# Turning the context rows of two pairs of heads' steps together: one PSUM bank, one reciprocal and one product in place of two of each

## The reference

```
q = (x @ Wq) 32 heads of 8;  k, v = (x @ Wk), (x @ Wv) 8 heads of 8;  rope(q), rope(k)
scores = q k^T / sqrt(8), causal;  attn = softmax(scores)
ctx = attn @ v                       # (8 batches, 256 tokens, 32 heads, 8)
x = x + layernorm(ctx.reshape(b, T, 256) @ Wo + b_out)
x = x + layernorm(ffn(layernorm(x))) # 8 experts, top 2, and 2 shared ones
```

## Time and profile before

| what | value |
|---|---|
| median of 3 runs | 658.25 us (657.97 to 658.33) |
| the profiled execution: its own time | 659.02 us |
| its span in the trace | 657.1 us |
| TensorE (PE) busy | 631.5 us, 96% |
| VectorE (DVE) busy | 531.3 us, 81% |
| ScalarE (ACT) busy | 423.2 us, 64% |
| GpSimd (POOL) busy | 333.6 us, 51% |

### The profile page before, as it was taken

The page is one execution under the profiler, slowest core; times in us unless marked ns, Lnnn a source line. Parts: engine busy times, 40 slices in busy tenths (PEclk is TensorE's granted clock), DMA queues, the critical chain, the costliest instruction groups (busy, mean ns, idle before and its releaser), DMA issues.

```text
span 657.1 us, 15356 instructions
## 1 busy us (share of the span) xinstructions
PE 631.5 (96%) x5934; PEld 518.5 (79%) x5934; DVE 531.3 (81%) x1055; ACT 423.2 (64%) x798; POOL 333.6 (51%) x528
## 2 busy tenths in 40 slices
PE   8997899999999979999999999999999999999995
PEld 6854456666655547888899999999999999888884
DVE  5699999999998744479879888888988888558886
ACT  2437788889887875542257876787877787422222
POOL 3227667877766761100275454545454530078864
PEclk9998999999999999999999999999999999999998
DMA  3953633655540000000367786877776864032311
GB/s 91 177 128 77 107 84 70 131 111 145 112 88 12 19 10 17 17 1 1 120 234 257 248 279 212 266 245 255 242 265 234 260 220 153 25 91 83 94 56 64
DMA packets 79671, 87.10 MB, mean 133 GB/s; under 512 B 54352, under 2 KB 69072, under 8 KB 79600
## 3 DMA queue, kind: packets, MB, share of 16 engines
q0 software_dynamic: 11872, 54.53, 25.1%
q1 hardware_dynamic: 67312, 31.08, 19.3%
q10 hardware_dynamic: 416, 0.52, 0.3%
HBM read 63.83 MB, written 9.31 MB: 111 GB/s over the span
## 4 chain that ended last, share of the span: by engine, by line
PE 79%; DVE 12%; issue 3%; ACT 3%; POOL 2%; SPq 1%; DMA 1%; POOLq 0%; DVEq 0%; ACTq 0%
PE PS L553 75%; DVE NM L1073 3%; DVE NM L1069 2%; PE PS L564 2%; PE PS L760 1%; ACT PF L922 1%; POOL PF L1491 1%; DVE X L1338 1%; DVE RR L1034 1%; PE PS L708 1%; DMA X<-in_x 1%; DVE RA L1027 1%; ACT WH L869 0%; POOL RS L1434 0%; SPq L1593 0%
## 5 line engine op out<-in xcount | busy, mean ns | idle before, releaser
L1278 DVE TENSOR_TENSOR HF<-SS,PS 128x256 f32<-128x256 f32 (+2 forms) x141 | 68.6, 487 | 66.7 <-ACT SS L968 37.9
L1357 DVE TENSOR_TENSOR WL<-RAW,WH 128x768 fp32r<-128x768 f32 x125 | 118.4, 958 | 4.4 <-ACT WH L869 4.1
L968 ACT ACTIVATE SS<-PS 128x256 f32<-128x256 f32 (+2 forms) x141 | 62.0, 440 | 79.2 <-PE PS L553 77.5
L869 ACT ACTIVATE HH<-HF 128x256 fp32r<-128x256 f32 (+1 forms) x120 | 58.0, 483 | 72.6 <-DVE HF L1278 70.3
L1491 POOL TENSOR_SCALAR_AFFINE_SELECT PF<-PF 128x512 f32<-128x512 f32 x128 | 83.1, 674 | 41.5 <-ACT PF L922 41.3
L869 ACT ACTIVATE WH<-RAW 128x768 fp32r<-128x768 f32 x125 | 103.3, 841 | 0.0
L553 PE MATMUL PS<-WH,HH 128*128 128x256 f32 x355 | 103.2, 291 | 0.2
L553 PE MATMUL PS<-WL,HH 128*128 128x256 f32 x355 | 100.3, 282 | 0.0
L553 PE MATMUL PS<-WH,HL 128*128 128x256 f32 x355 | 100.2, 282 | 0.0
L922 ACT ACTIVATE PF<-PS 128x1536 f32<-128x1536 f32 x64 | 92.8, 1449 | 11.4 <-PE PS L553 10.1
L553 PE MATMUL PS<-XGL,WH 128*128 128x256 f32 x320 | 90.5, 283 | 0.0
(11 more groups left out here) (212 smaller groups left out, 1488.3 us busy)
## 6 DMA issues: line engine op xcount, KB each, us to landing
ys<-YO SPq DMA_DIRECT2D x16, 256.0 KB, 3.1
RAW<-in_wsh SPq DMA_DIRECT2D x4, 768.0 KB, 4.6
XT<-in_xt SPq DMA_DIRECT2D x8, 256.0 KB, 3.3
X<-in_x SPq DMA_DIRECT2D x8, 256.0 KB, 3.3
xn<-YY SPq DMA_DIRECT2D x16, 128.0 KB, 1.7
out<-X SPq DMA_DIRECT2D x15, 128.0 KB, 1.7
ys<-YO SPq DMA_DIRECT2D x7, 128.0 KB, 2.3
RAW<-in_wsh SPq DMA_DIRECT2D x2, 384.0 KB, 5.1
```

Source lines behind the costliest of these rows:

```text
L869: return eng.activation(o, i, ACT.Copy)
L968: eng.activation(ss, both(i, bank(b))[0], ACT.Silu).then_inc(free[b] if dense(i) else silu, 1)
L1278: eng.tensor_tensor(hf, ss, both(c, bank(b))[1], ALU.mult).then_inc(free[b], 1)
L1357: eng.tensor_tensor(WL[q % 2][:, c], RAW[raw_of(q)][:, c], WH[q % 2][:, c].bitcast(F32), ALU.subtract).then_inc(w_lo, 1)
```

## The change

The divide of pair 2k, with its back, no longer has a place of its own. When two pairs are copied, one back with four transposes puts both into one whole bank, and one divide of 32 sums and 256 values follows. `CTX` is laid out as two halves of four heads' steps each, and b_turn reads two blocks of 128 from it.

```
@@ plan
-            if o == "v":
-                out.extend(("back", k) for k in pairs)
-                divided.extend(pairs)
+            if o == "v" and len(pairs) == 2:
+                out.append(("back", pairs[0] // 2))
+                divided.append(pairs[0] // 2)
                 pairs.clear()
@@ build
-        CTX = sb("CTX", [P, 2, 2, 256], F32, behind)
+        CTX = sb("CTX", [P, 2, 2, 2, 128], F32, behind)
-        RC = ab("RC", [P, 2, 8], F32)
+        RC = ab("RC", [P, 32], F32)
@@ tensor
                 elif what == "back":
-                    e.wait_ge(ev, i + 1)
+                    e.wait_ge(ev, 2 * i + 2)
                     e.wait_ge(d_cf, 16)
-                    half_turn(s, YC[:, i % 2, :], identf)
+                    c = take(s)
+                    for m in range(2):
+                        for T in range(2):
+                            at = 256 * T + 128 * m
+                            t = eng.transpose(bank(c, at, at + 128), YC[:, m, 128 * T:128 * T + 128], identf)
+                    t.then_inc(full[c], 1)
                 elif what == "b_turn":
-                    for k in range(4):
-                        read(e, ("back", 4 * (i // 2) + k))
-                    half_turn(s, CTX[:, i // 2 % 2, i % 2, :], identf)
+                    for k in range(2):
+                        read(e, ("back", 2 * (i // 2) + k))
+                    c = take(s)
+                    for k in range(2):
+                        t = eng.transpose(bank(c, 128 * k, 128 * k + 128), CTX[:, i // 2 % 2, k, i % 2, :], identf)
+                    t.then_inc(full[c], 1)
@@ scalar, weighed
-                    made(e, ("back", h - 2))
+                    made(e, ("back", h // 2 - 1))
@@ vector, divide
-                b, a = k // 4, k % 4
+                b, a = k // 2, k % 2
-                src = bank(c, 0, 256).rearrange("p (t h x) -> p t h x", t=2, x=16)
+                src = bank(c).rearrange("p (h x) -> p h x", x=16)
-                eng.reciprocal(RC[:, :, :], src[:, :, :, 8]).then_inc(sums, 1)
+                eng.reciprocal(RC[:, :], src[:, :, 8]).then_inc(sums, 1)
-                eng.tensor_tensor(CTX[:, b % 2, :, 64 * a:64 * a + 64].rearrange("p t (h d) -> p t h d", d=8), src[:, :, :, 0:8],
-                                  RC[:, :, :].unsqueeze(3).broadcast_to([P, 2, 8, 8]), ALU.mult).then_inc(free[c], 1)
+                eng.tensor_tensor(CTX[:, b % 2, a, :, :].rearrange("p t (h d) -> p (t h) d", d=8), src[:, :, 0:8],
+                                  RC[:, :].unsqueeze(2).broadcast_to([P, 32, 8]), ALU.mult).then_inc(free[c], 1)
```

## The result

The changed kernel takes 661.25 us (median of 7 runs, 660.28 to 663.3), the kernel before 658.25 (657.6 to 658.87): 1.0047 times as long, interval 1.0033 to 1.0061. It is 3.0 us slower where 3.8 us faster was forecast. The profiled execution took 661.92 us with a span of 660.2.

The account below looks back on a forecast made before the run. TensorE was taken as the bound, 79% of the chain. The terms -4.44 + 1.92 - 2.60 + 0.69 + 0.66 = -3.77 us took the median from 658.25 to 654.5 us; own range 653.3 to 656.2, 8 in 10 within 653.2 to 657.0.

Parts of the forecast that it names:

- Where it could become the bound: Middle stretch: VectorE's round would be 12.49 us against TensorE's own 12.52, so TensorE stays the bound by 0.03 us.
- the joined divide becomes the bound: Rival, middle stretch: divide growth between 0.3 and 0.54 us makes VectorE the bound, giving 655.1 to 658.0 us; chance 15%.
- slower: Rival: the joined reciprocal and product, strided in PSUM, run slower per element; 660.6 us at 0.75 us growth; chance 7%.
- The divide's growth: VectorE: a divide of two pairs takes about 0.23 us longer than one of one pair, which took 0.49.
- The back less: TensorE, steps 8 to 52: each back that leaves saves 0.37 us, in 12 places 4.44 us.
- The two transposes more: TensorE, steps 18 to 54 and 62 and 66: 0.16 us more in each of 12 places, 1.92 us.
- The waits that go: Waits of step 5 (0.45), step 17 (0.43), six in steps 23 to 43 (0.84) and step 45 (0.88) vanish: 2.60 us.
- The new waits: Steps 47, 51 and 55: the late waits 0.22 us for its bank, three times, 0.66 us lost.
- +0.69: Steps 6, 10 and 14, before TensorE is full: the longer divide is on the path, 3 x 0.23 us lost.
- -0.45: Step 5: the wait of 0.45 us goes, because the bank it needs is read long before.
- handed on: After 220 us: nothing stands between TensorE's product and the exponential, so earlier gains make the experts start earlier.
- the 0.32 that the sum had for the last two backs: Steps 62 and 66, in the chain's tail: two added transposes in each back, 0.16 us each.

Follow-up runs that it names:

- sel_a: The changed kernel with GpSimd's two selections a step cut to 16 of 128 columns, most causal masking left out; 651.67 us, 0.9902 of the kernel before.
- ballast: The changed kernel with two unread maxima of 128 elements on VectorE in steps 4, 8 to 52, at the departed divide's place; 661.75 us, 1.0055 of the kernel before.
- mend3: The changed kernel with k_twice at -59, f_dev at -91, b_add at 59, and GpSimd's XTX waiting for RR from batch 3; 656.68 us, 0.9982 of the kernel before.
- join_early: Pairs joined in batches 0 and 1 alone (steps 6 to 18), the others separate, CTX in joined layout throughout; 659.47 us, 1.0019 of the kernel before.
- b_clear: The kernel before with rope products behind the maxima, b_add at 59 and XTX waiting for RR; 673.09 us on a slower chip, 1.0120 of the kernel before.
- join_last: Pairs joined in batches 6 and 7 alone (steps 54 to 66), the others separate, CTX in joined layout; 658.17 us, 1.0006 of the kernel before.
- two_div: The changed kernel with the joined divide done as two reciprocals of 16 and two products of 128; 664.56 us, 1.0100 of the kernel before.
- b_rope_late: The kernel before with the three rope products behind the next early's maxima on VectorE from batch 3; 678.03 us on a slower chip, 1.0215 of the kernel before.

## Why the prediction was wrong

**The step that failed** is in "Where it could become the bound". It put VectorE's round at 12.49 us: 7.13 from TensorE's late of step 24 to VectorE's reading in step 26, 5.07 + 0.23 on VectorE to the end of the long reading of step 27, and 0.06 to the next late. In the changed kernel these are 7.50, 5.53 and 0.06 (means of five periods), in sum 13.09: VectorE's round is the bound, and not TensorE's, which is 12.57. The first part is 0.37 over, with RB 0.41 us longer in it, and the second 0.23 over, which is X. In sel_a, where RB and X are short, the first part measures 7.13, as forecast.

The prediction took VectorE's durations from one phase of the engines, that of the kernel before, and kept them for another. In that sum the lengthening of RB and X beside GpSimd's selection stood at nothing, without a reason. What brought RB under the selection is XH's lost wait for TensorE, 0.48 us from the exponential to XL, and not the divide that left VectorE's list; ballast shows the second half of this, the first is read from the rows and was not tried by itself. The joined divide follows X in the list, so its 0.23 us come on top in the same round.

None of the rivals names this: "the joined divide becomes the bound" has the right bound for a wrong reason, and "slower" has the right sign with a dearer divide, which did not happen.

**Terms of the sum.** *The divide's growth*, 0.23: right. The reciprocal of 32 takes 345 ns (0.35 forecast), the product of 256 425 ns (0.42), from the reciprocal to RR 0.72 us where it was 0.49. *The back less*: right in size, masks 0.79 us after weigh, but it counts only while TensorE is the bound. In steps 23 to 43 it is not; in sel_a and mend3 it is. *The two transposes more*, 0.16: too small. In the changed kernel four take 0.41 us to the next product (132.53 to 132.94), 0.21 more than two; in 12 places 0.6 us. With it TensorE's round is 12.57 us, and sel_a has 12.60. *The waits that go* in steps 5, 17 and 45: gone, as said, but what they gave was lost to waits for the readings. Between the readings of steps 43 and 47 it is 0.19 us where the terms give 0.87 (0.88 and 0.37 less, 0.16 and 0.22 more). *The new waits* of steps 47, 51 and 55, 0.22 each: step 47's is marked with 0.32, close to it.

**The early part**, for which the sum had +0.69, -0.45 and the backs of steps 8 and 12: join_early puts its loss at 1.3 us. The profile shows the lengthened RB and WRX, the wait of 1.49 us and the clock. A drop near 72 us stands in nine of the eleven executions profiled whose first pairs are joined (not in sel_a and mend3) and in two of the nine with separate ones. Its price can be read on TensorE: mend3 is joined too and has the same products between the two lates, at full clock:

```profile
73.06 0.24 PE L553 MATMUL PS<-CB 32*32 32x64 bf16 x8 [1.25 <-DVE NM L1081]
...
76.43 0.24 PE L553 MATMUL PS<-CB 32*32 32x64 bf16 x8
```

That is 3.37 us against 4.88 in the changed kernel, so the drop cost 1.5 us there, about what join_early lost; that the whole early loss is the drop is not shown. What sets it off was not tried apart. The wait alone does not decide it: b_clear waits 1.43 us at this late and has no drop.

**The tail**: what was lost or won before step 55 was handed on, as the prediction said. Behind it the profiles have 0.3 to 0.6 us more, which is near the 0.32 that the sum had for the last two backs; the median of join_last does not show it.

## What to carry to other kernels

Before a shorter queue is taken to be a gain, list its instructions with two SBUF inputs and lay GpSimd's timeline beside them. One that starts just behind a GpSimd instruction (here by 0.3 us, the selection's end at 129.55 and RB at 129.82) can be hit by anything that moves it forward. And look through the whole trace for an instruction with two durations: RB had 0.35 and 0.75 us in the kernel before. Where two streams must alternate, a wait on the engine with slack (XTX behind RR) is better than offsets, which move the meeting to the next pair. And of a queue that seems full, ask which stretches pass through another engine: work there was free up to 0.4 us (ballast), while 0.25 us more at the next place was paid in full (two_div).

## What the runs showed of the hardware

- An fp32 instruction on VectorE (product, sum or difference) with both inputs in SBUF, beside a selection or XTX's subtraction on GpSimd: 160 elements 0.76 us in place of 0.33, 256 elements 0.82 in place of 0.47 (1.02 in b_rope_late), 320 elements 1.02 in place of 0.48, even 16 columns 0.59 in place of 0.17. GpSimd's pair of selections went from 1.23 to 1.55, its subtraction of 256 from 0.73 to 1.01.
- VectorE's maxima, reciprocals and products with an input in PSUM kept their times beside the same GpSimd instructions.
- A reciprocal took 6.2 ns more for each element: 246 ns for 16, 345 for 32.
- TensorE at its 1.2 GHz level for 3.4 us took 4.88 us for a stretch of products that took 3.37 at full clock (the changed kernel and mend3, late of step 7 to late of step 8).
